# A recurrent cell's step: gate columns in three groups, one step per loop turn on TensorE, input gates put into the sums ahead

## The reference, cut to what matters

```
B, T, I, H, S = (64, 128, 512, 512, 4)        # sizes of the layer's own setup
i, f, g, o = split(gates, 4)
c_new = sigmoid(f) * c + sigmoid(i) * tanh(g)
h_new = sigmoid(o) * tanh(c_new)
# gates = x_t @ W_ih[s].T + h @ W_hh[s].T + b_ih[s] + b_hh[s], four cells s
# W_sel, b_sel choose the cell s of a step from (h, c, x_t)
```

## Time and profile before

| | |
|---|---|
| median of three runs | 7053.28 us (7048.97 to 7054.98) |
| the profiled execution | 7064.35 us, its span 7062.7 us |
| TensorE: busy share of the span, matmuls | 87%, 210539 |
| VectorE, ScalarE, GpSimd busy | 35%, 24%, 13% |
| granted TensorE clock, mean of the span | 0.956 |
| matmuls of 320 columns, `ps_rows` | 34944, 299 ns each |
| matmuls of 192 columns, `ps_rows_last` | 19968, 246 ns each |
| late matmuls, `ps_late` | 2496, 321 ns each |

### The profile page before, as it was taken

The page is one execution under the profiler, slowest core; times in us unless marked ns, Lnnn a source line. Parts: engine busy times, 40 slices in busy tenths (PEclk is TensorE's granted clock), DMA queues, the critical chain, the costliest instruction groups (busy, mean ns, idle before and its releaser), DMA issues. The chain is left out here.

```text
span 7062.7 us, 492288 instructions
## 1 busy us (share of the span) xinstructions
PE 6163.6 (87%) x210539; PEld 4094.5 (58%) x210539; DVE 2459.5 (35%) x11546; ACT 1721.2 (24%) x8472; POOL 928.5 (13%) x2082
## 2 busy tenths in 40 slices
PE   6856999999999999998779999999999999999852
PEld 5523555555555454554567777777777777777631
DVE  5324555555442211111233332333333332222248
ACT  0121333333333333333001111111111111111112
POOL 0011111111128810000000000000000000000003
PEclk9977999999999999999899999999999999999975
DMA  1011111111111100000232221222122221111100
GB/s 48 1 45 35 33 34 33 34 33 34 34 35 43 42 4 0 0 0 0 76 88 41 41 41 16 41 41 44 21 32 44 41 34 7 7 7 7 22 14 8
DMA packets 806866, 204.14 MB, mean 29 GB/s; under 512 B 701431, under 2 KB 766683, under 8 KB 806804
## 3 DMA queue, kind: packets, MB, share of 16 engines
q1 hardware_dynamic: 764500, 151.79, 11.3%
q0 software_dynamic: 41152, 46.42, 2.4%
q10 hardware_dynamic: 1152, 5.15, 0.2%
HBM read 174.86 MB, written 28.16 MB: 29 GB/s over the span
## 5 line engine op out<-in xcount | busy, mean ns | idle before, releaser
L1757 PE MATMUL ps_rows<-whh,h_pair 128*4 128x320 f16 x34944 | 1307.2, 299 | 85.1 <-issue 3.4
L1074 PE MATMUL ode_busy<-ode_busy_x,ode_busy_w 128*32 128x320 f16 (+4 forms) x19248 | 1247.9, 321 | 9.3 <-PEq L1010 7.1
L1757 PEld LDWEIGHTS ps_rows<-whh,h_pair 128*4 128x4 f16 x34944 | 735.5, 84 | 512.5 <-DVE h_pair L1615 154.0
L1068 PEld LDWEIGHTS ode_psa<-ode_a,ode_w2t 128*32 128x32 f32 x19968 | 397.6, 108 | 769.1 <-ACT ode_a L1183 572.3
L1627 DVE COPY gate_rows<-ps_rows_last 128x192 f32<-128x192 f32 x624 | 223.1, 358 | 1514.3 <-PE ps_rows_last L1757 1514.3
L1193 DVE SCALAR_TENSOR_TENSOR ode_part<-ode_b 128x1 f32<-128x1 f32 x624 | 112.6, 180 | 1647.9 <-ACT ode_b L1185 1647.9
L1679 ACT COPY gate_rows<-ps_rows 128x320 f32<-128x320 f32 x624 | 265.8, 426 | 1678.8 <-PE ps_rows L1757 1678.8
L1068 PE MATMUL ode_psa<-ode_a,ode_w2t 128*32 128x1 f32 x19968 | 606.8, 181 | 47.8 <-ACT ode_a L1177 43.1
L1185 ACT ACTIVATE ode_b<-ode_psa 128x1 f32<-128x1 f32 x2496 | 427.4, 171 | 814.3 <-PE ode_psa L1068 797.6
L1801 PE MATMUL ps_gates<-l_gsel,gate_rows 128*32 128x4 f32 x19968 | 397.4, 176 | 147.4 <-DVE gate_rows L1627 147.2
L1757 PE MATMUL ps_rows_last<-whh,h_pair 128*4 128x192 f16 x19968 | 521.7, 246 | 0.0
(11 more groups left out here) (505 smaller groups left out, 9528.1 us busy)
## 6 DMA issues: line engine op xcount, KB each, us to landing
late_w<-in_wih_t SPq DMA_DIRECT2D x386, 128.0 KB, 2.1
xg_buf<-xg_scratch SPq DMA_DIRECT2D x1248, 16.0 KB, 2.0
split_raw<-in_whh_t SPq DMA_DIRECT2D x64, 256.0 KB, 2.6
ig_w<-in_wih_t SPq DMA_DIRECT2D x8, 2048.0 KB, 11.6
xg_scratch<-late_out SPq DMA_DIRECT2D x24, 624.0 KB, 3.2
whh<-h_scratch SPq DMA_DIRECT2D x90, 62.5 KB, 2.4
xg_scratch<-ig_out ACTq DMA_DIRECT2D x8, 628.0 KB, 8.2
h_scratch<-mlp_h SPq DMA_DIRECT2D x40, 125.0 KB, 2.3
```

The lines of the kernel that those rows point to most:

```text
L1068: m = nc.tensor.matmul(ps[32 * j:32 * j + 32, 0:1], w[:, 32 * j:32 * j + 32], col, start=start, stop=stop, skip_group_check=True)
L1074: nc.tensor.matmul(ps_busy[32 * j:32 * j + 32, 0:cols], busy_w[:, 32 * j:32 * j + 32], busy_x[:, 0:cols], start=True, stop=True, skip_grou ...
L1757: m = nc.tensor.matmul(out[32 * j:32 * j + 4, :], hpair[:, c, 2 - 2 * part:6 - 2 * part], whh[:, at + lo:at + hi], start=(part == 0 and c ...
```

## The change

The gate columns are laid out anew: a 128-column block b now holds one gate, in the order i, g, f, o, with the four quarters of the state on the four partition groups. So columns 0 to 255 (i and g) are the first group, 256 to 383 (f) the second and 384 to 511 (o) the third, each with its own sum in PSUM (`ps_rows`, `ps_rows_forget`, `ps_rows_out`) and its own copy and counter. The output gate has a target bank of its own (`psq`) and a tanh of its own (`out_gate_tanh`); the first tanh covers the 12 columns of i, f and g.

The input gates are no longer put into `ps_gates` by matmuls with the identity: ScalarE copies them into both banks, in its branch, ahead of its copy of the rows. All the turning matmuls add to that.

TensorE's loop holds one step. Both late pieces of a step stand at its end, behind the turning of the output gate and the input's part of the next logits; they add to a sum that VectorE zeroes (a memset of `ps_late`), and their column address is computed from the loop's counter. `late_w` has half its size, one buffer, so each step's load must land before the next step's late pieces. `xsel_now` has one column, too; GpSimd refills it once `best` tells that the logits made from it are done.

```diff
@@ -1509,37 +1508,41 @@
-    FIRST = 5 * 64
+    FIRST = 2 * 128
+    IFG = 3 * KC
...
-        xgb = sb("xg_buf", [128, UN, 2, CELLS * 8])
+        xgb = sb("xg_buf", [128, UN, CELLS * 16])
...
-        act = sb("gates_and_c", [128, 20])
-        ccur = act[:, 16:20]
+        act = sb("gates_and_c", [128, 4 * KC])
+        ccur = act[:, IFG:IFG + KC]
+        out_tanh = sb("out_gate_tanh", [128, KC])
...
-        psg = ctx.enter_context(nc.psum_tensor("ps_rows", [128, CELLS * BANK], F32))
-        psb = ctx.enter_context(nc.psum_tensor("ps_rows_last", [128, BANK], F32))
-        psc, psl = (ctx.enter_context(nc.psum_tensor(n, [128, BANK], F32)) for n in ("ps_gates", "ps_logits"))
+        psg = ctx.enter_context(nc.psum_tensor("ps_rows", [128, CELLS * FIRST], F32))
+        psf, pso = (ctx.enter_context(nc.psum_tensor(n, [128, BANK], F32)) for n in ("ps_rows_forget", "ps_rows_out"))
+        pscq = ctx.enter_context(nc.psum_tensor("ps_gates", [128, 2, BANK], F32))
+        psc, psq = pscq[:, 0, 0:16], pscq[:, 1, 0:16]
+        psl = ctx.enter_context(nc.psum_tensor("ps_logits", [128, BANK], F32))
...
-                                load_late(g, quad + 1)
+                                load_late((g + 1) % UN, quad + (g + 1) // UN)
...
-                    nc.vector.scalar_tensor_tensor(parts[:], act[:, 0:8], 1.0, act[:, 12:20], ALU.add, ALU.mult).then_inc(S["fi"], 1)
-                    nc.vector.tensor_scalar(ok[:], act[:, 8:12], 1.0, 1024.0, ALU.add, ALU.mult).then_inc(S["o"], 1)
+                    nc.vector.scalar_tensor_tensor(parts[:], act[:, 0:2 * KC], 1.0, act[:, 2 * KC:4 * KC], ALU.add, ALU.mult).then_inc(S["fi"], 1)
                     v.wait_ge(S["fi"], k + 1)
                     nc.vector.scalar_tensor_tensor(ccur, parts[:, KC:2 * KC], 0.5, parts[:, 0:KC], ALU.mult, ALU.add).then_inc(S["c_ready"], 1)
+                    v.wait_ge(S["out_acted"], k + 1)
+                    nc.vector.tensor_scalar(ok[:], out_tanh[:], 1.0, 1024.0, ALU.add, ALU.mult).then_inc(S["o"], 1)
+                    nc.vector.scalar_tensor_tensor(wgated[:], out_tanh[:].unsqueeze(2).broadcast_to([128, KC, PAIRS]), 1.0, wsel[:, 0:KC, :], ALU.add, ALU.mult).then_inc(S["w_ready"], 1)
...
-                    v.wait_ge(S["kept"], k * 2)
+                    v.wait_ge(S["kept"], k * 2 + 1)
                     v.sem_inc(S["seen_v"], 1)
-                    v.wait_ge(S["rows_last"], k)
-                    nc.vector.tensor_copy(gsb[:, FIRST:D], psb[:, 0:D - FIRST]).then_inc(S["evac_v"], 1)
+                    v.wait_ge(S["rows_forget"], k)
+                    nc.vector.tensor_copy(gsb[:, 256:384], psf[:, 0:128]).then_inc(S["evac_f"], 1)
+                    v.wait_ge(S["rows_out"], k)
+                    nc.vector.tensor_copy(gsb[:, 384:512], pso[:, 0:128]).then_inc(S["evac_o"], 1)
...
+                            v.wait_ge(S["late_moved"], o * QUADS + quad + 1)
+                            v.sem_inc(S["seen_v"], 1)
+                            nc.vector.memset(ps_late[:, 0:BLOCK], 0.0)
...
-                    nc.scalar.activation(act[:, 0:16], psc[:, 0:16], ACT.Tanh).then_inc(S["acted"], 1)
+                    nc.scalar.activation(act[:, 0:IFG], psc[:, 0:IFG], ACT.Tanh).then_inc(S["acted"], 1)
+                    a.wait_ge(S["out_gate"], k + 1)
+                    nc.scalar.activation(out_tanh[:], psq[:, IFG:16], ACT.Tanh).then_inc(S["out_acted"], 1)
...
+                            nc.scalar.copy(pscq[:, :, 0:16], xgb[:, q, e * 16:(e + 1) * 16].unsqueeze(1).broadcast_to([128, 2, 16])).then_inc(S["xg_used"], 1)
                             a.wait_ge(S["rows_first"], k)
-                            nc.scalar.copy(gsb[:, 0:FIRST], psg[:, e * BANK:e * BANK + FIRST]).then_inc(S["evac_a"], 1)
+                            nc.scalar.copy(gsb[:, 0:FIRST], psg[:, e * FIRST:(e + 1) * FIRST]).then_inc(S["evac_a"], 1)
...
+                def next_input(k):
+
+                    g.wait_ge(S["best"], k + 1)
+                    g.sem_inc(S["seen_g"], 1)
+                    nc.gpsimd.tensor_copy(xcol[:], xsel[:, ds(k + 2, 1)]).then_inc(S["kept"], 1)
...
-                        g.wait_ge(late_in[1 - q], job * 16 + (16 + 16 * q * ahead))
+                        g.wait_ge(late_in, job * (16 * UN) + (16 + 16 * (q + 1) * ahead))
                         g.sem_inc(S["seen_g"], 1)
-                        nc.gpsimd.tensor_copy(xcol[:, q:q + 1], xsel[:, ds(k + UN, 1)]).then_inc(S["kept"], 1)
-
...
+                def logits_of_input():
+
+                    nc.tensor.matmul(psl[0:1, 0:PAIRS], xcol[:], pairs[:], start=True, stop=False, skip_group_check=True)
...
+                    return products(e, part, c, psg[:, e * FIRST:(e + 1) * FIRST], 0, FIRST, part == 0 and c == 0 and e % 2 == 0)
...
+                            m = products(e, part, c, psf[:, 0:128], 256, 384, (part, c) == (0, 0))
+                    m.then_inc(S["rows_forget"], 1)
+                    for part in range(2):
+                        for c in range(KC):
+                            m = products(e, part, c, pso[:, 0:128], 384, 512, (part, c) == (0, 0))
+                    m.then_inc(S["rows_out"], 1)
+
+                def turned(out, block_no):
+
+                    for j in range(4):
+                        m = nc.tensor.matmul(out[32 * j:32 * j + 32, :], gsb[:, block_no * 128 + 32 * j:block_no * 128 + 32 * j + 32], gsel[:, int(block_no == 1), :],
+                                             start=False, stop=True, skip_group_check=True)
+                    return m
...
+                    pe.wait_ge(S["hp_ready"], k)
+                    for c in range(AHEAD):
+                        for e in range(CELLS):
+                            first(e, 0, c)
+                    pe.wait_ge(S["best"], k)
+                    pe.sem_inc(S["seen_pe"], 1)
+                    s = pe.value_load(code[0:1, 0:1])
...
+                    pe.wait_ge(S["evac_a"], k)
+                    turned(psc[:, 0:KC], 0)
+                    turned(psc[:, 2 * KC:3 * KC], 1)
+                    pe.wait_ge(S["evac_f"], k)
+                    turned(psc[:, KC:2 * KC], 2).then_inc(S["gates"], 1)
+                    pe.wait_ge(S["evac_o"], k)
+                    turned(psq[:, IFG:16], 3).then_inc(S["out_gate"], 1)
+                    logits_of_input()
+                    for n in range(PER):
+                        m = nc.tensor.matmul(ps_late[:, 0:BLOCK], late_w[:, n * 128:(n + 1) * 128], xt_all[:, ds(late_at[n], BLOCK)], start=False, stop=True, skip_group_check=True)
+                    m.then_inc(S["late_used"], 1)
...
+                    with pe.Fori(0, UN * TURNS) as r:
+                        step(pe.snap(o * (UN * TURNS) + r + 1), [pe.snap((r % UN) * (PER * N) + (token + n * N)) for n in range(PER)])
```

More of the change, by code:

```diff
@@ L1402, in layer_mean @@
         stage_add(nc, "sage", x, [xn])
[L1405 to L1406 removed]
+BLOCK_GATE = (0, 2, 1, 3)
 QUADS = CELLS * 16
@@ L1748, in turn_of_two @@
[L1748 removed]
+                            if (part, c) >= (0, AHEAD):
+                                m = first(e, part, c)
+                    m.then_inc(S["rows_first"], 1)
+                    for part in range(2):
                         for c in range(KC):
[L1750 to L1751 removed]
```

165 lines of the change are left out of this document (68 added, 97 removed).

## The result

The changed kernel takes 7075.23 us (median of 7 runs, 7067.22 to 7080.6) against 7053.28 us for the one before (7 runs): ratio 1.0031, 95% interval 1.0020 to 1.0041. It is slower by some 20 us; I had forecast 7040 us, faster by 14. Its profiled execution took 7067.22 us (span 7065.6), 8 us under its median, where that of before was 11 over its own; so the two profiles differ by only 3 us, and I compare steps, not spans. The two traces come to the recurrent stage at different times, before at 3604.9 us and after at 3597.0 (the first reduce); from the first reduce to the last it takes 3072.3 us before and 3082.6 after, 10 us more.

A forecast was written before the change was run, and what follows sets the result against it. TensorE's in-order work, in a circle through the winner, was taken to bound the step: 1.13 + 1.72 + 0.39 + 1.07 + 0.59 = 4.90 us against 4.917, over 624 steps and less 3 us, -14 us: 7040 us, range 6965 to 7130.

The forecast's parts named there:

- TensorE's order: TensorE does its work in order, so its circle through the winner sets the step: 4.90 us against 4.917.
- the state's way: Circle from h_pair through rows, copy, turning and gates back to h_pair: 4.93 us, to shrink by 0.6 to 0.7.
- Term a: Start of VectorE's reduce to the winner's first weights: 1.13 us, bounds 1.05 and 1.20.
- Term b: TensorE's rows after the winner: 6 quads of 256 columns, 8 of 128, the last 8 and one duration: 1.72 us.
- Term c: End of the rows through VectorE's copy of the output block and back to TensorE: 0.39 us.
- Term d: Release of the last turning products to the first logit products of c: 1.07 us, bounds 0.98 and 1.15.
- Term e: 16 logit matmuls on TensorE, 0.55 us, and 0.04 to the reduce: 0.59 us.
- The start: First steps: code of the second copy of a step isn't loaded any more, -3 us.
- Edits at zero: Memset of ps_late, late sum's move, xg_buf's loads and the late load were taken to cost nothing, hidden in gaps.
- rival 3: Single buffer of late weights makes VectorE's copies and TensorE wait in 384 steps: at 0.2 each +77, 7115 us; 9%.
- Rivals 1, 2 and 4: In order: winner's way hidden, 6770 us, 7%; small quads not below 0.083, 7310, 7%; TensorE's clock halves, over 7700, 3%.

The follow-up runs named there:

- e2: Changed kernel without its late matmuls (calls dropped, counter raised instead; their weights still loaded): 6851.69 us, ratio 0.9706.
- e12: Changed kernel with the late matmuls' x_t addresses no longer dependent on the step's parity, one register instruction less (output partly wrong): 6964.56 us, ratio 0.9873.
- e1: Changed kernel with TensorE's loop unrolled to two steps again, single late buffer kept: 12715.6 us, ratio 1.8011.
- e6: Changed kernel with forget and output blocks in one group of 256 columns and TensorE's loop unrolled to two steps: 7074.37 us, ratio 1.0025.
- e10: Changed kernel with TensorE's loop of two steps, three groups of rows in the first and two in the second: 7026.9 us, ratio 0.9954.
- e5: Changed kernel with forget and output blocks in one group of 256 columns, loop of one step kept: 7167.31 us, ratio 1.0153.
- e9: Changed kernel with input logits before the output copy's wait and one late piece before the quads ahead, with its own half buffer: 7217.12 us, ratio 1.0226.
- e15: Changed kernel with the edge of TensorE's loop moved between the rows and the turning products: 7085.14 us, ratio 1.0045.
- e3: Changed kernel with 12 quads ahead of the winner instead of 8: 7135.16 us, ratio 1.0110.

## Why the prediction was wrong, step by step

- **TensorE's order bounds the step, and the 0.6 us that the state's way loses turn into idle time before the winner's weights.** Right: 0.55 us of "issue" there, h_pair ready 0.15 before the rows. The rows start 0.26 before the reduce, not 0.15. The state's way of 4.3 was never measured alone; the estimate from e2 is 4.35.
- **Term a,** 1.13: measured 1.10. Right.
- **Term b,** 1.72: 1.73. Small quads at 0.056: right, for 32 matmuls in 0.62 less 0.22 are 0.013 apart. The Trainium skill, in TensorE: Matmul & The Clock Gate, section "Wait — 56ns, not 53.3ns?", says that start to start never drops below about 25 ns. Across four column tiles this trace doesn't agree with it.
- **Term c,** 0.39: 0.395. Right.
- **Term d, 1.07: measured 1.115. This is the step that failed.** The prediction took 0.73 us from the first late matmul to the next weight load, in which the sequencer's work was to be hidden, and so left 0.34 for what stands in front; it gave the loop's branch only to the upper bound of 1.15. The part in front was right, 0.345. The part behind was 0.772, for count, branch and the next step's number end later than the late matmuls leave room: in the changed kernel c's logits stand 0.05 behind the end of the last register instruction. So the overlap was wrong, by 0.04 us. How near the edge this chain is, "one register instruction more, which is 0.05 to 0.11 long", hid from me: it is 0.129 long, takes 0.19 with its hand-over (3.28 to 3.47), and d is 0.94 without it (e12) and 1.115 with it. So 0.17 us a step, 107 us in all, hang on it; I took 0.09 more than before for all of d, and it was 0.135. Since the total rested on a difference of 0.017 us between two sums near 4.9, this 0.045 turned its sign.
- **Term e,** 0.59: 0.595. Right. The terms measured add up to 4.936, 0.036 over my 4.90: d gives 0.045 and b 0.01 too much, a 0.03 too little.
- **The start,** -3 us: first four steps 27.9 instead of 28.7 us. Nearly nothing.
- **Edits at zero.** ScalarE's copy, the move and the memset cost nothing seen. The single late buffer (rival 3) does make VectorE wait in some steps (0.12 us more before the forget block's copy in one of twenty), but steps with and without a load are equally long, 4.94 us. Rivals 1, 2 and 4 didn't come: the clock is 1.00 again, where the earlier trace rows had it, though TensorE idles more (2718.73 us busy of 3040).

```profile
3640.00:6680.00 3040.00, 2718.73 (x107205) 2251.24 (x107197) 1248.04 (x6581) 691.21 (x3080) 231.75 (x1232) 1.00 0.19 28
```

- What no term held: three groups need the loop of one step (e1), so what this loop costs is the price of the third group: -0.17 and +0.16 a step. The remainder is in e6 against the kernel before, +0.026 a step.
- **The range.** 7075 us lies inside the 6965 to 7130 that I gave, and slower had 39 in 100 beside 43 for faster. That is due to the width of the bounds and not to a right account of d: 1.15 was the case in which the branch isn't hidden, and the sum went by 1.07.

## What to carry to other kernels

Where an engine's order is the bound, write its sequencer's instructions into the circle too, each with start and end. An address computed in front of matmuls delays them (0.13 us here for one instruction); count and branch behind them are hidden only as long as the matmuls handed over last (0.73 us here), and a second branch cost 0.35. When a wait is put down to another engine, look whether that engine had long been done: in e2 the profile named c, and it was the sequencer. Before a loop body is made longer, look at the packets of the instruction queue: past the size that stays loaded, the cost is not per cent but a factor. Where a register read decides the next work, keep what stands ahead of it on its engine short in number of instructions, not only in time.

## What the runs showed of the hardware

- A loop body of 1752 weight loads and matmuls on TensorE is fetched again in each pass, 8.9 packets of 16.4 KB (e1); one of 1496 isn't (e10). The step is 14.0 us in the one and 4.86 in the other.
- VectorE's copies of 128 columns, 0.29 us long each, start 0.20 us apart when nothing is between them (e5).
- TensorE's sequencer: from the start of the register read to the winner's first weights, over two branches, 0.74 us in the changed kernel and 0.75 in e9; the loop's edge (count, branch, next number) 0.47 (e15) to 0.51 us to the end of its last register instruction, and 0.05 more to the next weights.
- With 32 matmuls ahead the sequencer's wait for the winner ends 0.20 us behind the start of the reduce, 0.04 behind its end, so it was there in time; with 48 (e3) only at 0.44, which is 0.70 behind the first of their weight loads.
